# A routed feed-forward layer's second batch: each fetch of a slot's weights starts when the one ahead of it has landed

## The reference, cut to what matters

```python
x = x + _L0_attn_ref(_layernorm(x), ...)        # attention, 16 heads, x is (2, 1024, 128)
# _L0_ffn_ref on h = _layernorm(x):
indices_s = argmax(gates, axis=1); scores = max(gates, axis=1)
for e in range(8):
    mask = (indices_s == e)
    hid = gelu(h @ w1[e] + b1[e])               # 128 -> 512
    out = out + mask * (hid @ w2[e] + b2[e])    # 512 -> 128
out = out * scores[:, None]
x = x + out
x = x + _L1_attn_ref(_layernorm(x), ...)        # conv, selective state recurrence
x = x + _L1_ffn_ref(_layernorm(x), ...)         # dense experts
```

## Time and profile before

| | us |
|---|---|
| median of 3 runs | 1136.53 |
| lowest, highest | 1133.59, 1137.57 |
| the profiled execution, its own time | 1136.75 |
| its span | 1135.4 |
| PE busy in the span | 1083.2 (95%) |
| DVE, POOL, ACT busy | 827.2, 760.6, 628.8 |
| DMA packets' share of 16 DMA engines, main queue | 18.8% |

### The profile page before, as it was taken

One profiled execution on the slowest core, in us unless ns is written; L12 is line 12 of the kernel. 1 busy time (PEld: TensorE's weight loads), 2 busy tenths in 40 slices (PEclk: granted clock), 3 DMA queues, 4 the chain that ended last, 5 costly groups with the idle time before them and its releaser, 6 DMA issues.

```text
span 1135.4 us, 18464 instructions
## 1 busy us (share of the span) xinstructions
PE 1083.2 (95%) x6858; PEld 650.1 (57%) x6858; DVE 827.2 (73%) x1226; ACT 628.8 (55%) x896; POOL 760.6 (67%) x394
## 2 busy tenths in 40 slices
PE   8999999999999999999999999869789987899998
PEld 4555655655655655565565656767444434445786
DVE  6875776676775775666976648325899999997987
ACT  4453555554544645554454554447986555757653
POOL 5688789688787797677789850330589796995200
PEclk9999999999999999999999999979899999999999
DMA  7000000000000000000000333466464444440000
GB/s 210 1 2 2 1 2 2 2 2 2 2 2 1 2 2 2 1 2 1 6 7 6 97 123 113 117 201 187 158 205 166 135 165 142 136 158 28 10 10 19
DMA packets 55369, 68.91 MB, mean 61 GB/s; under 512 B 23248, under 2 KB 41424, under 8 KB 55280
## 3 DMA queue, kind: packets, MB, share of 16 engines
q1 hardware_dynamic: 52272, 64.65, 18.8%
q0 software_dynamic: 1024, 2.10, 0.6%
q10 hardware_dynamic: 1984, 0.98, 0.3%
HBM read 61.30 MB, written 6.16 MB: 59 GB/s over the span
## 4 chain that ended last, share of the span: by engine, by line
PE 79%; issue 7%; DVE 5%; POOL 4%; ACT 2%; DMA 1%; another core or an unknown queue 1%; POOLq 0%; DVEq 0%; ACTq 0%
PE psum L658 20%; PE psum L619 16%; PE psum L644 6%; PE psum L676 5%; PE psum L632 5%; PE psum L1035 4%; PE psum L941 3%; PE psum L1018 3%; POOL hc L2213 3%; PE psum L733 3%; PE psum L691 2%; PE psum L799 2%; PE psum L810 2%; PE psum L713 2%; DVE psum L1884 1%
## 5 line engine op out<-in xcount | busy, mean ns | idle before, releaser
L2125 POOL TENSOR_TENSOR psums<-psums,prob 128x1024 f32<-128x1024 f32 x180 | 427.7, 2376 | 26.1 <-POOL psums L2125 0.5
L1594 DVE TENSOR_REDUCE mx<-psum 128x2 f32<-128x1024 f32 x256 | 300.3, 1219 | 128.2 <-PE psum L644 120.3
L1134 ACT ACTIVATE prob<-psum 128x1024 f32<-128x1024 f32 x256 | 261.4, 1027 | 62.8 <-PE psum L632 37.9
L658 PE MATMUL psum<-prob,V 128*64 128x512 f32 x1024 | 244.6, 599 | 0.0
L2213 POOL TENSOR_TENSOR hc<-hs,cc 128x1024 f32<-128x1024 f32 x64 | 151.4, 2366 | 21.0 <-DVE hs L1891 18.4
L1891 DVE TENSOR_TENSOR_SCAN hs<-dA,psum 128x1024 f32<-128x1024 f32 x64 | 146.3, 2287 | 2.2
L2125 POOL TENSOR_TENSOR psums<-prob 128x1024 f32<-128x1024 f32 x30 | 72.1, 2405 | 99.3 <-ACT prob L1134 99.3
L658 PEld LDWEIGHTS psum<-prob,V 128*64 128x64 f32 x1024 | 66.3, 136 | 109.5 <-issue 105.5
L941 PE MATMUL psum<-hc,ident 128*128 128x512 f32 x256 | 121.3, 596 | 2.9 <-DVE slot_rows_h L1899 1.4
L644 PE MATMUL psum<-k_hi,q_hi 64*128 64x512 f32 x512 | 107.2, 410 | 1.8 <-DVE mx L1594 1.3
L619 PE MATMUL psum<-q_hi,k_hi 64*128 64x512 f32 x512 | 106.3, 403 | 0.0
(11 more groups left out here) (298 smaller groups left out, 1687.2 us busy)
## 6 DMA issues: line engine op xcount, KB each, us to landing
cc<-C_rows SPq DMA_DIRECT2D x64, 512.0 KB, 3.7
kq_wts<-in_e_rows SPq DMA_DIRECT2D x14, 578.0 KB, 4.4
e_wts<-in_e_rows SPq DMA_DIRECT2D x10, 578.0 KB, 4.0
e_w<-in_e_rows SPq DMA_DIRECT2D x6, 578.0 KB, 5.1
slots_in<-e_zero SPq DMA_DIRECT2D x2, 960.0 KB, 7.1
inv<-sum_rows SPq DMA_DIRECT2D x120, 1.0 KB, 2.0
slots_out<-e_y SPq DMA_DIRECT2D x30, 64.0 KB, 2.1
e_w<-in_e_w SPq DMA_DIRECT2D x1, 1024.0 KB, 7.9
```

Source lines behind the costliest of these rows:

```text
L658: ins = pe.matmul(A.O[HALF[s], :], A.V[pair % 2][:, j, s * DH:(s + 1) * DH], A.prob[unit(pair, c, j) % NPB][:, s * CH:(s + 1) * CH], start ...
L1134: act.activation(A.prob[n % NPB][:, :], slots.bank("score", pair, c, j).rearrange("p s n -> p (s n)"), ACT.Exp, scale=float(DH) ** -0.5).t ...
L1594: dve.tensor_reduce(K.A.mx[:, :, t, c], slots.bank("max", pair, t, c), AXX, ALU.max).then_inc(*slots.inc("max", pair, t, c))
L2125: pool.tensor_tensor(total[:, :], (K.A.prob[(n - 1) % NPB] if j == 1 else total)[:, :], K.A.prob[n % NPB][:, :], ALU.add).then_inc(*K.psum ...
```

## The change

The fetch of slot `n` of the second batch (15 and up) gets one more wait, on the count that the fetch of slot `n - 1` raises on landing. The wait stands after the fetch's other waits and ahead of the load of the owner; nothing else is changed.

```diff
         sp.wait_ge(*K.work.full.at("turn", 1, FETCH_TURN[n]))
+    if n >= NSLOT:
+        sp.wait_ge(R.ld_wts[BUFFER[n - 1]], 16 * (USE[n - 1] + 1))
     row = sp.value_load(R.owneri[b][0:1, j:j + 1], min_val=0, max_val=(E0 - 1) * P)
     sp.dma_start(R.wts[BUFFER[n]], R.rows_d[bass.ds(row, P), :]).then_inc(R.ld_wts[BUFFER[n]], 16)
```

## The result

The changed kernel takes **1152.18 us** in the median of 4 runs (1151.41 to 1154.37), against 1137.05 (1133.59 to 1138.0, 4 runs) of the kernel before on the same chip: a ratio of **1.0143**, 95% interval 1.0130 to 1.0156 (the ratio on record; the two medians alone give 1.0133). The medians are 15.1 us apart, where 14.8 us were forecast (1151.3). Its profiled execution took 1152.69 us, with a span of 1151.4 where it was 1135.4. One run of this whole study, of the filled waits, took 2192.31 us; it is slow in a way that no other is, and no comparison uses it.

The account below looks back on a forecast made before the run. TensorE (PE) was taken as the bound, 79% of the chain of waits. Up 29 late by 12.9 us plus 1.9 us of lower clock makes 14.8 us, so 1151.3 us; range for 8 in 10 1145 to 1158.

Parts of the forecast that it names:

- One link: From one fetch's issue on SP to the next: lone landing 3.85 us plus 0.82 us to the issue, 4.67 us.
- Fetches 19 to 21: Start of the serial fetches: fetch 20 delayed half a microsecond, fetch 21 issued at 764.8 where it was 762.62.
- Up 29: Last up on PE: its weights land at 806.0 where it started at 793.13, 12.9 us on the path.
- The clock behind up 29: PE's work after up 29: one slow start at the lower clock after idling, 1.9 us, bounds 0 and 7.
- Fetches 15 to 18 at no cost: First four new waits on SP: over within 0.2 us or long before, covered by time between landing and use.
- The stores and the spreading of C: SP's transfers queued behind the waits: they go out later, moving with ups and downs, at no cost of their own.
- Short links: Rival: a lone fetch lands in 2.5 us, a link is 3.3 us, time stays 1136.7; 0.05 together with no-effect wait.
- Late clock: Rival: starved PE stays at the lower clock through L887 and the tail, about 21 us more, 1158; chance 0.13.
- The stall goes: Rival: spacing fetches frees up to 4.3 us of ACT's standstill at 758.17, about 1149; counted inside the forecast's 0.72.
- The wait does nothing: Rival: each count is reached before SP comes to it, time stays 1136.7; 0.05 together with short links.
- PE's waits: Sign in the profile after: PE waits for DMA before ups 25, 26, 27 and 29, two to four us each.
- The formula of the Trainium skill: Alternative landing estimate, 2.0 us fixed plus bytes at 436 GB/s: 3.36 us, link 4.18, sum 10.4 us, about 1147.

Follow-up runs that it names:

- the filled waits: Changed kernel plus 6 to 12 identity matmuls on PE while it waits for weights of slots 24 to 27 and 29: 1148.4 us (1.0147), then 1151.63 us (1.0139).
- two in flight: Changed kernel with each new wait on the fetch two ahead instead of one: 1132.73 against 1132.42 us of the kernel before, ratio 1.0005.
- the waits of 21 to 29: Changed kernel with the new wait only at fetches 21 to 29, none at 15 to 20: 1145.32 us, ratio 1.0118 to the kernel before.
- the first four waits: Changed kernel with the new wait only at fetches 15 to 18: 1134.43 against 1132.42 us of the kernel before, ratio 1.0018.
- fetch 17 behind the stores: Kernel before, without new waits, fetch 17 placed on SP behind the stores of slots 12 to 14: 1135.82 against 1136.62 us, ratio 0.9993.

## Why the prediction was right, point by point

- **The bound.** Right. PE's chain through the routed part set the end, and every microsecond by which up 29 came later arrived at the end. By the medians the sum of 14.8 us is met closely here (15.1), but it is nearer than its terms are: the two profiled spans lie 16.0 us apart, and on two other chips the change cost 16.9 and 17.1. All of these lie within 0.1 us of the forecast's 11 to 17 us.
- **One link.** 4.67 us forecast, 4.65 measured over eight links; landings 3.6 to 3.9 where 3.85 was taken, 0.78 from landing to issue where 0.82 was taken. One of the two fetches called alone was not quite: fetch 27 lands at 786.04 and fetch 28 is issued at 785.10. The 4.0 us read from it held all the same as the upper bound. The kernel with the owner loaded first shows both terms apart, and the one with two in flight shows that nothing else in the wait costs.
- **Fetches 19 to 21.** The term that was too small. Fetch 21 was forecast 2.2 us later than before, at 764.8. It came at 765.20, which looks close, but this execution stood 1.0 us earlier at up 15: against that mark it was 3.6 us later. The half microsecond given to fetch 20 was 2.0 at its landing (764.42 after, 763.42 before, against the same mark). With the waits of 15 to 20 taken out, fetch 21 went out 13.4 us after up 15, where the changed kernel on that chip had 15.4.
- **Up 29.** 12.9 us forecast; 13.1 by the clock on the wall, 14.1 against up 15, inside the bounds of 11.0 to 14.7.
- **The clock behind up 29.** 1.9 us forecast, 1.7 measured in all three profiles of the changed kernel, and absent in both profiles with work in PE's waits. It was absent too in one profile without such work (the waits of 21 to 29), and in unprofiled times it was not confirmed. So its mechanism holds, but which instructions the lower clock meets varies, and the closeness of 1.7 to 1.9 is partly luck.
- **Fetches 15 to 18 at no cost.** No cost is seen in the first chip's traces, but on another chip this step was wrong: there the four waits cost 2.0 us. It took the spacing of 4.66 us between fetches 16 and 17, and a landing within 4.0, from one trace; on that chip the spacing was 3.16 and the landing 4.76. And it looked at the fetch and its up, not at the three stores behind it, for which the gathers wait; that the late gathers are what costs is argued, not shown.
- **The stores and the spreading of C.** Right. POOL stands still for 1.31 us before the first product in both profiles, with DVE as what ends it. The chain that ended last does run through the spreading of C after the change, but its first transfer landed at 821.86, 1.0 us ahead of the product at 822.83, and the product came 3.66 us after POOL's instruction before it, as it did before the change (3.65).
- **The rivals.** *Short links* fell: no landing of the nine from fetch 21 on was under 3.6 us (fetch 20, at the hole, took 3.14). *Late clock* did not come: the clock fell in short pieces between 785 and 811, not throughout, and up 28 ended (804.10) before fetch 29 landed (806.19). *The stall goes* fell: ACT's hole there was 3.8 us in both first profiles, and it was absent on two chips in kernels with and without overlapping fetches. *The wait does nothing* fell with SP's waits, which now name the buffers (28.5 us in all, 25 to 30 forecast; three rows, by the memories of the buffers):

```profile
SPq L2319 <- DMA kq_wts<-in_e_rows: 13.4, 5, 3.0
SPq L2319 <- DMA e_w<-in_e_rows: 8.4, 3, 3.1
SPq L2319 <- DMA e_wts<-in_e_rows: 6.7, 3, 3.1
```

- **PE's waits.** Forecast before ups 25, 26, 27 and 29, two to four us each; measured 2.68, 1.21, 2.95 and 2.13. There was one before 24 as well, 1.56 us. The prediction's own formula has fetch 24 land at 782.66, half a microsecond after up 24 started in the kernel before (782.16), so this wait was overlooked; it landed at 782.55, and PE was there earlier.
- **What the sum did not have.** The first product to the last took 1.0 us more. It isn't put down to the change: kernels as fast as the one before (the first four waits, two in flight, fetch 17 behind the stores) have 227.5 to 227.8 us there as well, against 226.7 in the one profile of the kernel before, and the filled waits 226.4. The gap of 1.0 at up 15 has the other sign, and the two cancel, which flatters the total.
- **The formula of the Trainium skill.** The estimate of 3.36 us for a transfer of this size, from the Trainium skill's page "DMA: Bandwidth & Descriptors", section "Anatomy of one DMA — SWDGE (gpsimd) path", would have made the sum 10.4 us. That section fits transfers issued on GpSimd's path, which the prediction left out; these fetches are issued from SP. The landings of 3.6 to 3.9 us decide here.

## What to carry to other kernels

When transfers that used to overlap are made to wait for each other, count one link as the landing of a lone transfer plus all that the issuing engine does between the wait and the issue, multiply by the number of transfers, and compare only the last landing with its use. In this kernel allowing two in flight cost nothing, and moving the register load ahead of the wait took 0.5 us from every link. And look at what is queued behind a waiting instruction even where the wait is short: three small stores behind a fetch were what another engine was waiting for. A spacing read from one trace, such as the 4.66 us between two fetches, may be another on the next chip.

## What the runs showed of the hardware

The holes until 738.8 and from 758.2 us in the earlier trace rows are not an effect of the change. In each of the two traces of the first chip ACT stood still twice, for 8.4 us in all, with nothing named as the cause. On two other chips (kernels before at 1132.4 and 1132.0 us) there was no such hole, in seven kernels of this study, the changed one among them. On the third (1136.6 us) they were back in all four kernels, the second one 3.3 to 6.6 us long. ACT's waits in the changed kernel on that chip, from 730 to 770 us:

```profile
ACT slotT L1228 <- remote: 5.6, 1, 5.6
ACT slot_rows_h L1240 <- remote: 4.7, 1, 4.7
```

and PE's in the changed kernel on a chip without them, from 728 to 770 us, where the transfer of rows and DVE's rows take the place of ACT:

```profile
PE psum L786 <- DMA slot_rows_h<-slots_in: 5.7, 1, 5.7
PE psum L600 <- DVE xrows L1566: 3.9, 1, 3.9
```

Where the holes are, each begins while a burst of eight indirect transfers from POOL is still being issued and ends 1.6 to 1.9 us after the last of them, and some of SP's short instructions then take 0.7 us (in the kernel before one at 737.95 and five from 758.78 on). The same bursts leave no hole on the other two chips. The kernel before was 4 to 5 us faster there, about the size of one hole; that the holes are the reason isn't shown. What causes them stays open; a kernel without the bursts was not tried. The first four waits cost 2.0 us on a chip without holes, and on chips with them the traces show none of that, so a single trace doesn't settle what hides a wait.
